# Attention kernel of three transformer layers: the row maxima enter the transposed scores as two further rows of the queries, placed by small DMAs

## What is computed

```
qkv = h @ W_qkv + b_qkv
q, k, v = (qkv[:, :, 0], qkv[:, :, 1], qkv[:, :, 2])
scores = jnp.einsum('blhd,bmhd->bhlm', q * scale, k)
attn = jax.nn.softmax(scores, axis=-1)
o = jnp.einsum('bhlm,bmhd->blhd', attn, v).reshape(b, l, c)
return o @ W_proj + b_proj
x = x + gate_msa * _attention(h, W_qkv, b_qkv, W_proj, b_proj)
```

## Time and profile before

| | us |
|---|---|
| median of 3 runs | 370.22 |
| lowest and highest run | 366.45, 371.04 |
| the profiled execution | 366.48 |
| its span | 364.7 |
| PE busy | 304.6 (84%) |
| DVE busy | 293.6 (80%) |
| ACT busy | 207.4 (57%) |
| POOL busy | 166.1 (46%) |
| mean granted clock of PE | 0.934 of full |

### The profile page before, as it was taken

One profiled execution on the slowest core, in us unless ns is written; L12 is line 12 of the kernel. 1 busy time (PEld: TensorE's weight loads), 2 busy tenths in 40 slices (PEclk: granted clock), 3 DMA queues, 4 the chain that ended last, 5 costly groups with the idle time before them and its releaser, 6 DMA issues.

```text
span 364.7 us, 10730 instructions
## 1 busy us (share of the span) xinstructions
PE 304.6 (84%) x3474; PEld 211.6 (58%) x3478; DVE 293.6 (80%) x1511; ACT 207.4 (57%) x460; POOL 166.1 (46%) x536
## 2 busy tenths in 40 slices
PE   1969964981748888799999999999898989989896
PEld 0924821570125355477878777777666666766675
DVE  4999999999994678878888888797989887887632
ACT  4146110252002355788888888887786876768552
POOL 5424332457543322535454645444746555462442
PEclk9999565898678999999999999999999998999999
DMA  4697300049200223241222222222120223222101
GB/s 145 190 247 233 123 1 0 4 86 308 89 1 0 47 44 74 44 59 36 58 44 45 47 47 46 45 45 46 29 44 18 47 45 45 43 32 45 34 18 34
DMA packets 49503, 23.58 MB, mean 65 GB/s; under 512 B 40954, under 2 KB 47966, under 8 KB 49320
## 3 DMA queue, kind: packets, MB, share of 16 engines
q1 hardware_dynamic: 49448, 22.89, 27.1%
HBM read 12.82 MB, written 0.62 MB: 37 GB/s over the span
## 4 chain that ended last, share of the span: by engine, by line
PE 43%; DVE 36%; issue 8%; DMA 4%; POOL 3%; SPq 3%; ACT 1%; POOLq 0%; DVEq 0%
PE ps L1017 36%; DVE grow L1643 4%; DVE nmax L1972 3%; DVE top L1698 3%; DVE trow L1643 3%; DMA skw_r<-brief 3%; PE ps L1411 3%; DVE beta L1677 2%; DVE den L1683 2%; DVE tfac L1691 2%; DVE late L1665 2%; DMA tmask<-in_tmask 2%; DVE lead L1665 1%; PE ps L1308 1%; DVE skw_r L2021 1%
## 5 line engine op out<-in xcount | busy, mean ns | idle before, releaser
L1972 DVE TENSOR_REDUCE nmax<-ps 128x4 f32<-128x512 f32 x96 | 63.4, 684 | 12.2 <-PE ps L1017 12.0
L797 ACT ACTIVATE skw_t<-ps 128x512 f32<-128x512 f32 x96 | 52.0, 595 | 15.3 <-PE ps L1017 14.7
L449 POOL TENSOR_TENSOR root<-grow,half 32x1 f32<-32x1 f32 x64 | 34.6, 542 | 53.6 <-DVE grow L1643 53.2
L1017 PE MATMUL ps<-skw_r 54*128 54x128 bf16 x768 | 43.6, 218 | 5.4 <-issue 2.0
L1017 PEld LDWEIGHTS ps<-skw_r 54*128 54x128 bf16 x768 | 30.8, 94 | 21.1 <-issue 16.1
L1017 PE MATMUL ps<-mT_t,fc1w_t 128*128 128x256 f32 (+1 forms) x130 | 36.0, 379 | 0.0
L1017 PE MATMUL ps<-fc2w,skw_r 128*128 128x144 f32 (+1 forms) x240 | 34.7, 292 | 0.0
L1017 PEld LDWEIGHTS ps<-fc2w,skw_r 128*128 128x128 f32 (+1 forms) x240 | 30.8, 190 | 1.6 <-issue 0.2
L1017 PE MATMUL ps<-sel,identb 128*128 128x512 bf16 x63 | 18.8, 423 | 12.0 <-DVE grow L1643 10.9
L1017 PE MATMUL ps<-nmT,sel 64*128 64x128 bf16 x384 | 28.0, 218 | 0.0
L814 ACT ACT_TABLE_LOAD x21 | 26.9, 1283 | 0.4
(11 more groups left out here) (273 smaller groups left out, 817.8 us busy)
## 6 DMA issues: line engine op xcount, KB each, us to landing
gmod<-spread_mods SPq DMA_DIRECT2D x3, 1408.0 KB, 13.2
adaw_t<-in_ada SPq DMA_DIRECT2D x3, 432.0 KB
tails<-in_tail SPq DMA_DIRECT2D x3, 427.1 KB
skw_r<-brief SPq DMA_TRANSPOSE x72, 2.5
skw_t<-in_skw SPq DMA_DIRECT2D x1, 1024.0 KB
fc1w_t<-in_fc SPq DMA_DIRECT2D x3, 320.0 KB
fc2w<-in_fc SPq DMA_DIRECT2D x3, 288.0 KB
qkvw_t<-in_qkv SPq DMA_DIRECT2D x3, 216.0 KB
```

The lines of the kernel that those rows point to most:

```text
L449: g.tensor_tensor(root[:, p, j:j + 1], grow[:, i % 4, 0:1], half[:], ALU.pow).then_inc(root_ready, 1)
L797: a.activation(prob[g].rearrange("p i t -> p (i t)"), ps[:, 2 + g % 2, :], ACT.Exp, scale=SCALE).then_inc(prob_ready, 1)
L1017: return pe.matmul(o, lhsT, rhs, start=start, stop=stop, skip_group_check=True)
L1972: d.tensor_reduce(nmax[:, v % 2, first:first + 7:2], ps[:, 6 + g % 2, :].rearrange("p (i t) -> p i t", i=4), AX_X, ALU.max, negate=True).t ...
```

## The change

**Two further rows.** The rows 54 and 55 of a head's 64 in `qkT` are now used. In the keys they hold 1.0: POOL's memset of the unused rows of `parts` writes 0.0 for the queries and 1.0 for the keys, and the transposes carry it along. In the queries SP writes the two parts of the maxima there, by two small DMAs of 16 pieces of 256 bytes each from `nmT` (`place_maxima`). `scores_T` multiplies 56 rows in one product where it had two, and waits for the semaphore `max_placed` in place of `nmT_ready`. `scores` goes on with 54 rows. The selector's product is gone.

**Ring of three.** `qkT` has a third buffer, in `skw_t`; SP and `q_out` wait for the `scores_T` of the visit three before. SP turns two visits ahead, then for each visit places its maxima and turns the visit after the next.

**Own orders.** The orders of the steps are written anew for all four computing engines. `fc1(m, 1)` goes from the end of an even slot to the start of the odd one, `second_deviation` (POOL) to the next slot, `q_out` and `input_variance` (DVE) from the end of a slot to the start of the next, `qkv` in the odd slots of the first two layers behind `scores_T(0)` and `scores(2)`, and `scores_T(0)` there behind `scores(0)`, half of fc2 and `proj`. Six warming products of slots 1 and 2 go, three are put ahead of the first `max_turn`.

```diff
@@ the block of SP
-            for v in range(VISITS):
+            def turn_visit(v):
                 h = v % 2
                 sp.wait_ge(parts_ready, v + 1)
-                if v >= 2:
-                    sp.wait_ge(sT_full, 4 * (v - 2) + 4)
-                sp.dma_start_transpose(qkT[1][h][:, 0:4, :], heads_of(1, h, 0)).then_inc(keys_turned[h], 16)
+                if v >= 3:
+                    sp.wait_ge(sT_full, 4 * (v - 3) + 4)
+                sp.dma_start_transpose(qkT[1][v % 3][:, 0:4, :], heads_of(1, h, 0)).then_inc(keys_turned[h], 16)
                 for k in range(2):
-                    sp.dma_start_transpose(qkT[k][h][:, 4:8, :], heads_of(k, h, 1)).then_inc(turned[h][k], 16)
+                    sp.dma_start_transpose(qkT[k][v % 3][:, 4:8, :], heads_of(k, h, 1)).then_inc(turned[h][k], 16)
+
+            def place_maxima(v):
+                h = v % 2
+                sp.wait_ge(nmT_ready, v + 1)
+                for half_ in range(2):
+                    at, row = 64 * half_, 64 * half_ + HROWS
+                    sp.dma_start(qkT[0][v % 3][row:row + 2, :, :], nmT[h][at:at + 16, :]).then_inc(max_placed[h], 16)
+
+            turn_visit(0)
+            turn_visit(1)
+            for v in range(VISITS):
+                place_maxima(v)
+                if v + 2 < VISITS:
+                    turn_visit(v + 2)
@@ the block of POOL
-                    g.memset(parts[(i - 57) // 2][(i - 57) % 2][:, :, HROWS:64], 0.0)
+                    g.memset(parts[(i - 57) // 2][(i - 57) % 2][:, :, HROWS:64], float((i - 57) // 2))
@@ the block of PE, scores_T
                 if g == 0:
-                    pe.wait_ge(nmT_ready, v + 1)
+                    pe.wait_ge(max_placed[v % 2], 32 * (v // 2 + 1))
                 for n in range(4):
                     for gg in (g, g + 1):
-                        _, (q, k) = operands(v, gg, n)
-                        mm(banks[gg - g][:, n * T:(n + 1) * T], k, q, True, False)
-                    for gg in (g, g + 1):
-                        i = mm(banks[gg - g][:, n * T:(n + 1) * T], *maximum(v, head_of(gg, n)), False, True)
+                        q, k = operands(v, gg, n, HROWS + 2)
+                        i = mm(banks[gg - g][:, n * T:(n + 1) * T], k, q)
                         if n == 3:
                             i.then_inc(sT_full, 1)
@@ the block of DVE, the order of odd slots of the first two layers
                     visit_at(residue, slot + 1, start=1)
-                    visit_at(max_high, slot)
+                    visit_at(max_low, slot)
                     visit_at(second_parts, slot + 1, start=1)
-                    visit_at(max_low, slot)
+                    pair_at(mlp_out, slot, 5)
                     visit_at(third_parts, slot + 1, start=1)
-                    pair_at(mlp_out, slot, 5)
                     visit_at(max_out, slot)
```

More of the change, by code:

```diff
@@ L604, in _ @@
                 if slot < 2 and slot % 2 == 0:
[L605 to L617, removed]
+                    pair_at(second_deviation, slot, 4)
                     visit_at(first_deviation, slot + 2, start=2)
@@ new lines, in _ @@
+                    visit_at(pv, slot - 1, 0)
+                    visit_at(o_back, slot - 2)
+                    visit_at(pv, slot - 1, 1)
+                    visit_at(pv, slot - 1, 2)
+                    visit_at(o_turn, slot - 2)
+                    visit_at(qkv, slot + 1, start=1)
+                    visit_at(scores, slot, 0)
+                    pair_at(fc1, slot, 4, 0)
+                    visit_at(pv, slot - 1, 3)
+                    visit_at(scores_T, slot - 1, 2)
+                    visit_at(scores, slot, 2)
@@ new lines, in _ @@
+                    visit_at(proj, slot - 2)
+                    pair_at(h2_turn, slot, 4)
+                elif slot < 2 and slot % 2 == 1:
+                    pair_at(fc1, slot, 5, 1)
+                    visit_at(parts_turn, slot)
+                    visit_at(o_back, slot - 2)
+                    visit_at(max_turn, slot - 1)
+                    pair_at(fc2, slot, 5, 0)
+                    pair_at(fc2, slot, 5, 1)
+                    pair_at(fc1, slot, 5, 2)
+                    visit_at(h_turn, slot + 1, start=2)
+                    visit_at(scores_T, slot - 1, 0)
+                    visit_at(proj, slot - 2)
+                    visit_at(scores, slot, 0)
+                    visit_at(qkv, slot + 1, start=1)
+                    visit_at(scores, slot, 2)
+                    visit_at(pv, slot - 1, 0)
+                    visit_at(scores_T, slot - 1, 2)
@@ L1445, in _ @@
                     visit_at(o_turn, slot - 2)
+                    visit_at(pv, slot - 1, 1)
                     visit_at(pv, slot - 1, 2)
                     visit_at(pv, slot - 1, 3)
-                    pair_at(fc1, slot, 4, 1)
+                elif slot >= VISITS - 1 and slot % 2 == 0:
+                    visit_at(max_turn, slot - 1)
+                    visit_at(h_turn, slot + 1, start=2)
+                    visit_at(o_back, slot - 2)
+                    visit_at(qkv, slot + 1, start=1)
+                    visit_at(scores_T, slot - 1, 0)
+                    visit_at(last_tail_turn, slot - 3, start=LAST)
+                    visit_at(scores, slot, 0)
+                    visit_at(o_turn, slot - 2)
+                    pair_at(h2_turn, slot, 4)
@@ L1457, in _ @@
                     visit_at(h_turn, slot + 1, start=2)
-                    visit_at(parts_turn, slot)
-                    pair_at(fc2, slot, 5, 0)
-                    visit_at(qkv, slot + 1, start=1)
-                    pair_at(fc2, slot, 5, 1)
-                    visit_at(max_turn, slot - 1)
-                    visit_at(proj, slot - 2)
-                    visit_at(scores, slot, 0)
-                    visit_at(scores_T, slot - 1, 0)
-                    visit_at(o_turn, slot - 2)
-                    visit_at(scores, slot, 2)
@@ L1506, in _ @@
[L1506 to L1507 removed]
                     pair_at(fc2, slot, 5, 0)
                     visit_at(scores, slot, 0)
[L1510 removed]
+                    pair_at(fc2, slot, 5, 1)
+                    visit_at(scores_T, slot - 1, 2)
+                    visit_at(last_turn, slot - 2, start=LAST)
                     visit_at(pv, slot - 1, 0)
[L1512 removed]
+                    visit_at(scores, slot, 2)
@@ L2302, in _ @@
                     visit_at(input_squares, slot + 3, start=2)
-                    visit_at(input_variance, slot + 3, start=2)
-                    visit_at(q_out, slot + 1)
 def kernel(**inputs):
```

454 lines of the change are left out of this document (217 added, 237 removed).

## The result

The changed kernel takes 496.24 us (median of 4 runs, 493.42 to 499.29), the kernel before 369.05 us in the same comparison: a ratio of 1.347, 95% interval 1.341 to 1.354. I had forecast 468 us in a range of 430 to 495. The direction and the place are as forecast, and so are the waits; the size lies just above the range.

The account below looks back on a forecast made before the run. PE bounds the first two layers, and PE and DVE share the third. The profiled 366.5 us plus 83.6 from the slots plus 18.7 for the clock is 468.8, forecast as 468, range 430 to 495.

Parts of the forecast that it names:

- The queue: On SP, each visit's placements issue behind the next visit's three transposes, which hold SP for 3.9 us.
- The walk through the slots: PE and DVE slot by slot: pairs 23.3 us for 17.6 in first two layers, 30.45 for 20.75 in third.
- The placement: Two small DMAs between the copy of nmT and scores_T: issue 0.41 us, landing 1.7, 2.3 in all if alone.
- The start: Slots before the steady pairs: third_parts(2) ends near 139 us, scores_T of visit 1 starts near 145, not 136.0: +9.
- The clock: PE at half clock 3.4 us after each stall, 1.7 lost: 11.9 in first two layers, 6.8 in third, +18.7.
- Costed at nothing: Ring of three and steps moved over slot edges: covered by new stalls; without stalls worth tenths of a us a pair.
- The removed products: On PE, 16 selector products a visit go: 0.93 us a pair off first two layers, about half in third.
- A: Rival: only the placements' latency counts, transposes not holding SP: +18, so 385 us, up to 404 if the clock falls; 8%.
- B: Rival, faster: placements land before PE comes to scores_T, so dropping 16 products a visit is the gain: 357 us; 3%.
- C: Rival: stalls as forecast, but PE's clock stays up: 450 us; 20%.
- D: Rival: each restart after a stall takes 5.3 us at half clock, 15 x 2.65 in place of 18.7: 490 us; 10%.

Follow-up runs that it names:

- run 1: Changed kernel without placements and with the old scores_T (eight more selector products a call) put back; ring of three and new orders stay: 383.12 us.
- run 2: Changed kernel without placements; scores_T keeps its one product, waits for the copy of nmT, and leaves the maxima out: 374.0 us.
- run 12: Changed kernel with placements issued from ACT's queue, and warming products ahead of scores_T in its shorter waits: 414.32 us.
- run 9: Changed kernel with warming products ahead of scores_T where PE stands still, including slots 1 and 23; placements stay on SP: 466.45 us.
- run 11: Kernel before, in its old orders, with the ring of three and the one product but no placements, maxima left out: 365.89 us.
- run 3: Changed kernel with each visit's placements ahead of the next visit's transposes in SP's queue: 456.85 us (one run).
- run 5: Changed kernel with placements issued from ACT's queue ahead of exps, SP left with the transposes alone: 435.97 us.
- run 6: Changed kernel with two further small DMAs, into rows nobody reads, issued by SP just ahead of each visit's placements: 525.95 us (one run).
- run 4: Kernel before, in its old orders, given only the placements, the one product and the ring of three: 509.89 us (one run).

## Why the forecast was right in kind and short in size

The runs split the loss like this. Own orders: +15.5 (run 1). One product: -9.1 in those orders (run 2 less run 1). Placements, their latency and ACT's share in it, with the clock mostly kept up: +40 (run 12 less run 2). SP's queue, the transposes ahead of the placements: +52 (run 9 less run 12). The clock: +30 (the changed kernel less run 9). Together 129 us, which is 496.24 less 367.57, the kernel before beside the first runs. The lines between them are not quite sharp. The first two depend on the order in which they are taken: the one product, with the ring, gains 2.2 us in the old orders (run 11), and the new orders then cost 8.1 (run 2 less run 11); only their sum, 6, is the same. Counted in stretches of 0.5 us as busy time times what is missing from a granted clock of 1, the changed kernel loses 50 us of PE time behind the rotation, run 12 loses 13, and runs 2 and 9 lose 6. So some 5 of the 40 belong to the clock.

Step by step:

- **The queue.** Right. Placements behind three transposes in all of the visits but the last, SP held for the whole of each bar. Runs 3, 5 and 6 move or load that queue, and the time follows. The Trainium skill, page "Perfetto Trace Analysis", section "DMA Instruction — HWDGE (DVE, Sync)", says that the interval shown for such a DMA ends when the sequencer is free for the next instruction. The trace agrees: 290.29 + 3.06 is 293.35, and the placement starts at 293.40, though its copy of `nmT` had ended at 292.44.
- **The walk through the slots.** Close, and too short by 16 us in all: run 9, with the clock kept up, takes 466 us against 450. Run 9 has S_e to S_o 12.45 us in the second layer (247.04 to 259.49; forecast 12.25), S_o to S_e 11.22 (11.05), and in the third layer 16.24 and 14.52 (15.95 and 14.5). Its stretches were forecast, at full clock, as 139, 26.8, 91.4 and 25.1, against 143.3, 29.6, 92.0 and 26.3: 9 of the 16 us. Most of the others are the start, below.
- **The placement.** The term was too small. An issue takes SP 0.61 us, not the 0.41 of `p_u`, though both move 16 pieces of 256 bytes. Landing was right: PE starts 1.9 us after the second issue, waking included, where I had 1.8. The rule is 6.45 us after `third_parts`, not 6.2: 0.25 at each of the 21 waits is 5 us, part of the 9 above.
- **The start.** Too small by 6 us: S_e of visit 1 is at 150.71, where I had 145. `third_parts(2)` ended at 144.30, not near 139. The clock isn't the reason: in run 9, with 16 warming products there, S_e is at 151.05. What makes `third_parts(2)` late was not traced.
- **The clock. This is the step that failed.** I counted 1.7 us for each restart, all of it in the first two layers (11.9) and half of it in the third (6.8), 18.7 in all; the runs show 29.8. The count of the stalls was right, 7 and 8. Stretch by stretch the changed kernel is longer than run 9 by 13.2, -0.4, 13.2 and 3.9 us, and by 0.9 in the end. So the first two layers pay 13, near my 11.9, and the third pays 17 in place of 6.8. "In the third I count half of it, beside DVE" is what was wrong: there PE loses 20 us of work to the half clock (counted as above, from slot 16 to slot 24), and the kernel is 17 us longer there: nearly all of it is on the path. I had also taken the length of the half clock from the shorter of two gaps in the trace of before (3.4 us, behind a wait of 1.65), although my stalls were to be 4 to 7 us long and the trace also had the longer gap, with 5.3 us at half. Behind the twelve waits of 5.7 us and more of the changed kernel it lasts 3.1 to 6.2 us, 4.8 in the mean, a loss of 2.4 each. At the start it cost next to nothing: the clock is at half from 136 us on, and still S_e comes no later than in run 9.
- **Neither alone.** With the clock's 29.8 in place of 18.7 the sum would be 480, with run 9's walk 485. It took both to leave the range, and by 1 us. The walk is short by more, 16 us, but of 84, in sizes; the clock is short by 11 of 30, and there the reasoning was wrong.
- **The orders.** "Costed at nothing" was wrong by 15.5 us if the stalls weren't there (8.1 beside the one product): 1.4 us a pair in slots 2 to 14, not tenths. With the placements it didn't show, since there the new orders are the better ones (run 4), as I had supposed.
- **The removed products.** Their size was right and their place wrong. In run 11 the call at 203.47 is over 0.33 us later (`o_back` at 203.80), where before it was 0.57 (222.72 to 223.29): 0.24 for eight products, 0.03 each. Over a pair the four calls save 0.24, 0.16, 0.02 and 0.24, 0.7 us. But PE's being the bound by 0.2 us (17.38 of 17.60) did not mean that 0.9 could come off. In the even slot PE now comes to `h2_turn` before POOL's tail is ready, and S_e waits for the transposed maxima. So 0.1 us a pair is left in the mean of four pairs, and 2.2 us in all. In the new orders the same products are worth 9.1 us: PE's busy time in a pair falls by 0.90 there (17.95 to 17.05), as I had it.
- **The rivals.** A, latency only, was the nearest to what run 5 tested, and its price of 385 to 404 was too low (436, of which 6 are orders and products, and 22 the clock); as an account of the change it is out. B's gain never was there to be had: even without placements it is 2 us, not 10 (against a kernel before of 368.13). C, the forecast with the clock kept up, is run 9: 466 against 450. D, 490, came nearest, but by luck: its clock costs 40 us, 10 more than was measured, and its walk, which is the forecast's, is 16 too short. Its length of the restart, 5.3 us, was nearer to the measured 4.8 than my 3.4, and it stood in my own rows; I gave it 10%.

What stays open is how the 40 us of the placements on ACT's queue divide. A pair of run 12 takes 21.5 to 21.6 us in the second layer, where run 2 has 17.5 to 17.9, and the trace shows two parts beyond the plain latency. In odd slots the placement starts 0.64 us behind its copy, in the third layer mostly 0.9 to 1.4, because ACT is not there yet. And from the first issue to PE's start, from slot 4 on, it is mostly 2.5 to 2.6 us in odd slots, but 2.7 to 3.8 in even slots of the first two layers, where SP issues its transposes at the same time:

```profile
249.22 0.23 DVE L2011 COPY nmT<-ps 128x128 bf16<-128x128 bf16 x1
249.48 0.62 ACTq L803 DMA_DIRECT2D skw_t<-nmT  x1
250.13 0.62 ACTq L803 DMA_DIRECT2D skw_t<-nmT  x1
253.30 0.40 PE L1037 MATMUL ps<-skw_t 56*128 56x128 bf16 x8 [1.30 <-DMA skw_t<-nmT]
```

That the transposes lengthen the landing is not shown: no run moved the two apart alone.

## What to carry to other kernels

A small DMA put between two engines costs no more than its latency only if nothing stands ahead of it in its queue (and here what was left with the queue and the clock out of the way was still 40 of 127 us), so price the whole queue between its trigger and its issue, transposes above all, and follow both orders of that queue before choosing. Where a change makes PE stand still for several us at a time, price the restart at half clock from the gap in the trace that is as long as the new stall, and don't halve it because another engine shares the bound: here 17 of 20 us were on the path where I had counted half. And before paying anything for a saving, measure it alone, in the kernel as it is: here it was 2 us.

## What the runs showed of the hardware that I had not expected

The issue of a placement, SBUF to SBUF with 16 pieces, holds its queue 0.61 us on SP and 0.62 on ACT, half as long again as the load `p_u` of the same shape (0.41). On ACT that need not take time from its arithmetic: in run 5 `h_out`, which stands ahead of the placements in ACT's order, ran from 231.96 to 232.58, beside the issues at 231.85 and 232.53.

A wait of the same length left the clock up once and brought it down the next time. In run 5 PE waited 2.77 us up to 191.89 and 2.76 us up to 212.83, each ahead of the same work of an even slot. The clock behind each (columns as in the earlier trace rows):

```profile
191.90:195.90 4.00, 3.78 (x41) 2.60 (x41) 2.22 (x9) 3.16 (x7) 1.20 (x5) 1.00 0.18 37
...
214.00:218.00 4.00, 4.00 (x29) 2.80 (x27) 1.97 (x8) 2.58 (x6) 0.55 (x1) 0.57 0.07 13
```

The wait's length alone does not say whether the clock falls, so for waits this short both cases belong into a range. For waits of 5.7 us and more there was no exception in the changed kernel: each of the twelve was followed by half clock. How long it lasted was no matter of the wait either. Behind waits of 5.89 and 5.88 us, one pair of slots apart, it was 5.7 and 3.6 us:

```profile
229.46:235.50 6.04, 6.04 (x40) 4.23 (x41) 1.94 (x8) 3.34 (x7) 0.55 (x1) 0.53 0.01 3
...
255.41:259.00 3.59, 3.59 (x17) 2.20 (x17) 1.21 (x6) 1.19 (x3) 0.55 (x1) 0.50 0.00 0
259.00:261.00 2.00, 1.85 (x26) 1.39 (x24) 1.04 (x3) 2.00 (x6) 0.00 (x0) 0.99 0.02 4
```

The pairs between 177.75 and 307.18 go with it: those behind the longer half clock take 26.0 to 26.5 us, those behind the shorter one 25.2 to 25.3, in turn, with the same work in them.
